# Moving one batch's last norm by half a step and splitting the final copy, turn, sum and store in two, in a one-core gated cross-attention and mixture-of-experts kernel

## What is computed

```python
x = x + tanh(g_xattn[0]) * attention0(layernorm(x), ctx)   # 16 heads of 8
x = x + tanh(g_ffn[0])   * quantised_linear(layernorm(x))  # Hadamard turn, 4-bit rows, ternary weights
x = x + tanh(g_xattn[1]) * attention1(layernorm(x), ctx)   # 16 heads of 64
x = x + tanh(g_ffn[1])   * experts(layernorm(x))           # 32 experts of width 64, top 4, plus a shared expert
```

## Time and profile before

| what | value |
|---|---|
| three runs, median (lowest to highest) | 264.85 us (264.17 to 266.33) |
| the profiled execution's own time | 264.59 us |
| its span in the profile | 262.9 us |
| busy: PE, DVE, ACT, POOL | 95%, 80%, 72%, 69% |
| granted TensorE clock, mean | 0.997 of full speed |

### The profile page before, as it was taken

How to read it: one execution, slowest core, us unless ns; L and a number is a source line. 1 busy time by engine, 2 the same in 40 slices (tenths; PEclk the granted TensorE clock), 3 DMA queues, 4 the chain that set the end, 5 groups by cost and what they waited for, 6 DMA issues and landing times.

```text
span 262.9 us, 6701 instructions
## 1 busy us (share of the span) xinstructions
PE 250.2 (95%) x1899; PEld 198.8 (76%) x1899; DVE 209.8 (80%) x652; ACT 189.0 (72%) x453; POOL 181.7 (69%) x272
## 2 busy tenths in 40 slices
PE   7897999999899999999999999999999999999995
PEld 5574668776667777768777888777887768999994
DVE  3999999999989896799677876777888623996863
ACT  2588899989899787857776767686787654556652
POOL 5667987998899675746744575439767795956661
PEclk9999999999999999999999999999999999999998
DMA  6557463400025566644485766756571051123510
GB/s 197 183 143 281 154 196 86 124 0 4 1 66 119 113 147 146 143 107 103 126 220 122 187 170 172 200 147 162 117 170 42 5 161 40 54 70 126 163 61 20
DMA packets 25475, 31.86 MB, mean 121 GB/s; under 512 B 4000, under 2 KB 18144, under 8 KB 25312
## 3 DMA queue, kind: packets, MB, share of 16 engines
q1 hardware_dynamic: 25008, 31.23, 44.4%
q10 hardware_dynamic: 432, 0.22, 0.3%
HBM read 14.32 MB, written 2.42 MB: 64 GB/s over the span
## 4 chain that ended last, share of the span: by engine, by line
PE 74%; DVE 14%; issue 6%; ACT 3%; DMA 1%; SPq 0%; DVEq 0%; ACTq 0%
PE bank L1325 18%; PE bank L1501 16%; PE bank L1330 6%; PE bank L1463 5%; PE bank L1332 5%; PE bank L1331 5%; PE bank L1464 5%; DVE masked L990 3%; PE bank L1516 3%; PE bank L1457 3%; DVE probsT L1007 2%; PE bank L1591 2%; DMA small<-in_L_ffn_weight 1%; PE bank L1594 1%; PE bank L1592 1%
## 5 line engine op out<-in xcount | busy, mean ns | idle before, releaser
L639 POOL TENSOR_SCALAR probs<-probs,rsum 128x512 f32<-128x512 f32 x128 | 88.3, 697 | 47.9 <-DVE rsum L999 47.3
L786 ACT ACTIVATE probs<-masked,neg_max 128x512 f32<-128x512 f32 x128 | 91.9, 719 | 7.4 <-DVE neg_max L990 7.1
L1325 PE MATMUL bank<-ident,probs 128*128 128x128 f32 x512 | 77.9, 275 | 2.0 <-ACT probsT L795 0.8
L1325 PEld LDWEIGHTS bank<-ident,probs 128*128 128x128 f32 x512 | 59.6, 141 | 15.3 <-issue 7.8
L990 DVE CUSTOM_DVE_ANT_0 masked<-bank,mask 128x512 f32<-128x512 f32 x64 | 43.8, 684 | 17.1 <-PE bank L1464 16.4
L795 ACT ACTIVATE probsT<-bank 128x512 f32<-128x512 f32 x76 | 45.0, 592 | 16.2 <-PE bank L1325 15.9
L1501 PE MATMUL bank<-probsT,val 128*32 128x256 f32 (+1 forms) x512 | 46.6, 384 | 0.0
L990 DVE CUSTOM_DVE_ANT_0 masked<-bank,shared 128x512 f32<-128x512 f32 x64 | 43.3, 677 | 0.8 <-PE bank L1457 0.4
L1007 DVE COPY probsT<-bank 128x512 f32<-128x512 f32 x52 | 35.2, 677 | 4.0 <-PE bank L1325 3.7
L1501 PEld LDWEIGHTS bank<-probsT,val 128*32 128x32 f32 (+1 forms) x512 | 24.4, 123 | 17.2 <-issue 4.2
L1457 PE MATMUL bank<-parts 128*128 128x512 f32 x64 | 31.2, 487 | 1.3 <-DVE neg_max L990 1.1
(11 more groups left out here) (266 smaller groups left out, 519.9 us busy)
## 6 DMA issues: line engine op xcount, KB each, us to landing
k_both<-k_low SPq DMA_DIRECT2D x32, 128.0 KB, 2.5
k_both<-k_high SPq DMA_DIRECT2D x32, 128.0 KB, 2.7
q<-q_split SPq DMA_DIRECT2D x32, 128.0 KB, 2.4
probsT<-staged_gate SPq DMA_DIRECT2D x32, 128.0 KB, 3.0
q<-q_split SPq DMA_DIRECT2D x32, 64.0 KB, 2.2
parts<-staged_k SPq DMA_DIRECT2D x7, 256.0 KB, 2.9
w_flat<-in_w SPq DMA_DIRECT2D x1, 1536.0 KB, 7.5
staged_q<-q_split SPq DMA_DIRECT2D x4, 256.0 KB, 2.6
```

The source lines that it names most:

```text
L639: pool.tensor_scalar(p, p, rsum[:, u % NCOL:u % NCOL + 1], 1.0, ALU.mult, ALU.mult).then_inc(normed, 1)
L786: act.activation(probs[:, u % NP, :], masked[:, u % NS, :], ACT.Exp, scale=-1.0, bias=neg_max[:, c:c + 1], accum_out=sums[:, c:c + 1]).the ...
L1325: ins = pe.transpose(dst[0:rows, t * P:t * P + P], src, ident[:, :])
```

## The change

In the router of batch 1, the norm's turn goes from n = 7 to n = 8, on PE between `up(4, 0)` and `up(4, 1)`, and the logits from n = 8 to n = 9, on PE behind `up(4, 1)` and `down(1)`. On ACT the norm's two copies go from before `high_hid(2)` to behind silu(4), ahead of `high_hid(3)`; the late exponentials stay at n = 10. On DVE `x1_low` goes from before `multiply(3)` to behind `hidden(3)`, and the selection from n = 9 (before `multiply(4)`) to n = 10 (behind `hidden(4)`). Rank and gate turn stay where they are.

At the end, the copy of 128x256 becomes two of 128x128, the turn two single transposes that each wait for their own half and write to two different banks, the sum two of 128x128, and the store two of 64 KB: the first from SP, the second from ACT's queue. The first batch's end is as before.

```diff
--- before.py
+++ after.py
@@ -106,8 +106,8 @@
 Y_DONE = {(k.layer, k.b): k.out_at + 1 for k in BLOCKS if k.g == k.groups - 1}
 
 
-LATE_JOBS = {"ln": 7, "logits": 8, "rank": 11, "turn_gate": 14}
-LATE_ROUTER = {3: (0, 1), 5: (3,), 9: (6, 10), 11: (11, 12)}
+LATE_JOBS = {"ln": 8, "logits": 9, "rank": 11, "turn_gate": 14}
+LATE_ROUTER = {3: (0, 1), 5: (3,), 10: (6, 10), 11: (11, 12)}
 
 
 HIDDEN_AT = {e: (e,) for e in range(2 * STEPS)}
@@ -591,9 +591,13 @@
                                  staged_gate[b, 2 * d:2 * d + 2, h, :].partition_broadcast(HID)).then_inc(gate_loaded[n % GATE_SLOTS], 16)
 
             def store(b):
-                sp.wait_ge(y_used, 3 + b)
-                sp.dma_start(out.rearrange("b (t p) d -> p b t d", p=P)[:, b, :, :],
-                             x_sb[:, NQ * b:NQ * b + NQ, :]).then_inc(stored, 16)
+                if b == 0:
+                    sp.wait_ge(y_used, 3)
+                    sp.dma_start(out.rearrange("b (t p) d -> p b t d", p=P)[:, b, :, :],
+                                 x_sb[:, NQ * b:NQ * b + NQ, :]).then_inc(stored, 16)
+                else:
+                    sp.wait_ge(y_used, 4)
+                    sp.dma_start(out[b, 0:P, :], x_sb[:, NQ * b, :]).then_inc(stored, 16)
 
             sp.wait_ge(job_done, jobs_done(range(8)))
             for b in range(B):
@@ -604,7 +608,7 @@
                     load_gates(b, d)
             for b in range(B):
                 store(b)
-            sp.wait_ge(stored, 16 * B)
+            sp.wait_ge(stored, 16 * (B + 1))
 
 
         @block.gpsimd
@@ -909,7 +913,11 @@
                 act.wait_ge(down_done, (b + 1) * STEPS)
                 if b:
                     act.wait_ge(y_turned, b)
-                act.activation(yT, moe_bank[b][:, 0:SQ], ACT.Copy).then_inc(yT_ready, 1)
+                if b == 0:
+                    act.activation(yT, moe_bank[b][:, 0:SQ], ACT.Copy).then_inc(yT_ready, 1)
+                else:
+                    for t in range(NQ):
+                        act.activation(yT[:, t * P:t * P + P], moe_bank[b][:, t * P:t * P + P], ACT.Copy).then_inc(yT_ready, 1)
 
             for b in range(B):
                 for p in range(HALVES):
@@ -924,9 +932,9 @@
                         if e >= 2:
                             act.wait_ge(hid_ready, e - 1)
                         act.activation(silu[:, e % 2, 0:wide], u_bank[e % 2][:, 0:wide], ACT.Silu).then_inc(silu_ready, 1)
-                        if n + 1 == LATE_JOBS["ln"]:
+                        if n == LATE_JOBS["ln"]:
                             job(("ln", 3, 1))
-                        if n == LATE_JOBS["logits"] + 2:
+                        if n == LATE_JOBS["logits"] + 1:
                             job(("logits", 1))
                         if n == LATE_JOBS["turn_gate"] - 2:
                             job(("turn_gate", 1))
@@ -936,6 +944,8 @@
                         copy_y(0)
             high_hid(2 * STEPS - 1)
             copy_y(1)
+            act.wait_ge(y_used, 5)
+            act.dma_start(out[1, P:SQ, :], x_sb[:, NQ + 1, :]).then_inc(stored, 16)
 
 
         @block.vector
@@ -1314,8 +1324,11 @@
                 dve.wait_ge(down_done, e + 1 - RING)
                 dve.tensor_tensor(hid_low[:, e % RING, 0:cols], hidT[:, e % RING, 0:cols], hid_high[:, e % RING, 0:cols].bitcast(F32),
                                   ALU.subtract).then_inc(last_low_ready, 1)
-            dve.wait_ge(y_turned, 2)
-            add_y(2, 1, 3)
+            for t in range(NQ):
+                x = x_sb[:, NQ + t, :]
+                dve.wait_ge(y_turned, 2 + t)
+                dve.scalar_tensor_tensor(out=x, in0=moe_bank[t][:, 0:P], scalar=tanh_g[:, 3:4], in1=x,
+                                         op0=ALU.mult, op1=ALU.add).then_inc(y_used, 1)
 
 
         @block.tensor
@@ -1599,7 +1612,12 @@
                 pe.wait_ge(yT_ready, b + 1)
                 if b:
                     pe.wait_ge(y_used, 3)
-                turn_tiles(moe_bank[0], [tmp[:, t, :] for t in range(NQ)]).then_inc(y_turned, 1)
+                if b == 0:
+                    turn_tiles(moe_bank[0], [tmp[:, t, :] for t in range(NQ)]).then_inc(y_turned, 1)
+                else:
+                    for t in range(NQ):
+                        pe.wait_ge(yT_ready, 2 + t)
+                        pe.transpose(moe_bank[t][:, 0:P], tmp[:, t, :], ident[:, :]).then_inc(y_turned, 1)
 
             for b in range(B):
                 for p in range(HALVES):
@@ -1617,6 +1635,9 @@
                         up(e, 0, u_bank, u_ready)
                     if n == HALVES:
                         down(QUADS - LAG, "both")
+                    if n == LATE_JOBS["ln"]:
+                        pe.wait_ge(*freed(("logits", 0)))
+                        job(("ln", 3, 1))
                     if p % 2 or p == PAIRS:
                         up(e, 1, v_bank, v_ready)
                         for done in HIDDEN_AT.get(e - LAG, ()):
@@ -1625,9 +1646,8 @@
                     if n == HALVES + 9:
                         turn_y(0)
                     for j in AFTER.get(n, ()):
-                        if j == ("ln", 3, 1):
-                            pe.wait_ge(*freed(("logits", 0)))
-                        job(j)
+                        if j != ("ln", 3, 1):
+                            job(j)
             for e in range(2 * STEPS - LAG, 2 * STEPS - 2):
                 down(e, "both")
             for part in ("high", "low"):
```

## The result

The changed kernel takes 266.18 us (median of 21 runs, 265.33 to 267.02); the kernel before, beside it, took 265.56 us (21 runs, 264.17 to 266.55). The ratio is 1.003, 95% interval 1.0017 to 1.0044: slower by 0.8 us (0.45 to 1.2), inside 1%. The forecast was 265.9 us, 1.05 us more than the median then known. The profiled execution took 266.5 us, its span 264.6 us (before 264.59 and 262.9).

What follows compares the result with a forecast made beforehand. TensorE, busy 95% of the span, was taken as the bound, so only its waits and the end count. 264.59 + 1.4 (router) - 0.35 (end) = 265.65, with 0.26 for the median 265.9 us; range 264.0 to 267.2.

Steps and rivals of the forecast that it cites:

- The late rank: Batch 1's router: the later selection makes the rank on PE start 1.7 us later, at 234.0 against 232.26.
- What comes back: Behind the rank: part of the delay is regained, leaving `multiply(5)`, `down(5)` and all after 1.4 us later.
- The bounds of 0.9 and 1.8: Lower and upper limits, in us, of the router move's forecast loss of 1.4 us.
- The norm's turn: Batch 1's router: PE turns 0.2 us later, ACT's copy `xnT` comes 1.8 us later; `down(1)` gets a new wait.
- The logits' wait: Batch 1's router on PE: the logits start at 229.75, behind a wait of about 0.35 us.
- The end: Halved copy, turn, sum and store: -0.35 us, 0.1 from an earlier last issue and 0.25 from half the data.
- The page's rule against two transfers: Last store: disjoint halves serialize on the same 16 engines, so the landing gains nothing; the end gives only -0.1 us.
- part 2: The kernel's end in halves: forecast -0.35 us, bounds -0.6 and +0.3.
- A: Rival at `down(2)`: the selection ends before PE is through, so the removed waits count; 263.9 us, chance 0.18.
- B: Rival at PE's idle stretch before the rank: the clock falls, costing 2.4 us more; 268.3 us, chance 0.09.
- C: Rival at the end: the second store on ACT's queue lands 1 us later than SP's; 267.1 us, chance 0.08.
- D: Router: smaller loss if the selection or `x1_low` get ahead; 265.2 us, counted inside the likeliest case's 0.65.

Runs made afterwards that it cites:

- rank_late: The changed kernel with the rank two halves later on PE, behind `down(3)`; measured 1.0032 (1.0015 to 1.0049) of the kernel before.
- end_stores_on_sp: The kernel before with the end in halves, both 64 KB stores issued from SP; one execution, 3.57 us from last copy to span's end, for 3.73.
- router_only: The kernel before with all the router's moves of the change and none of the end's; measured 1.0076 (1.0049 to 1.0104) of the kernel before.

## Why the prediction was right

- **The late rank.** Foretold 1.7 us late, with PE idle from 232.4 to 234.0; it was 1.70 us late with 1.40 us shown as idle. The 0.3 us that PE was to give back ahead of `down(5)` it did give back (0.28), but ahead of the gate turn and of `up(9, 0)`; at `down(5)` itself the spacing from the start before is 0.28 us in the old kernel and 0.27 in the new. The step carried because it followed the order of the three engines' lists and took the lengths (0.69 for a product, 2.29 for the selection) from rows.
- **What comes back.** Foretold 1.4 us at `multiply(5)` and `down(5)`; measured 1.40 and 1.42, and 1.44 for the router alone. That this is a bound of its own, and not what is left over from the first, is shown by rank_late. The bounds of 0.9 and 1.8 weren't needed.
- **The norm's turn.** The copy 1.8 us later for a turn 0.2 us later: 1.78 and 0.20. The new wait ahead of `down(1)` was there, 0.41 us shown. The logits' wait was to be about 0.35 us; the profile shows 0.20, and 0.37 beyond the usual spacing from start to start (0.48, less the spacing of 0.11 to 0.12).
- **The end.** The sum -0.35 held (-0.36), but its two terms were mis-sized in opposite directions. The work in halves was to give 0.1 us and gave 0.03, since the first turn starts 0.42 us behind the copy's start (261.65 - 261.23), where I had 0.32: if the first copy was over after 0.27, as I had it (the row shows both copies together), the handover from ScalarE to TensorE took about 0.1 us more than the 0.05 that I had read off the old copy. From there on the lengths were as foretold (0.61 us for both sums, foretold 0.62). The landing was to give 0.25; from the last issue's start to the end it gave 0.33, of which half the data alone is 0.28 (end_stores_on_sp). But that counts only because the second store could be issued at once: on SP it would have come 0.15 us later behind its data. That ACT's queue is worth 0.18 us in the tail wasn't in the prediction, which held it for a risk.
- **The page's rule against two transfers** (the Trainium skill, DMA: Bandwidth & Descriptors, Rules for kernel authors) would have made part 2 -0.1 us. That row speaks of halves by partition, while both stores here cover all 128 partitions, so it bears on this end only by its reason, that the two share the same engines. The trace differs from what I made of it: with the halves ready at different times two stores end 0.31 us sooner than one (3.39 against 3.70). That a second issuing engine saves issue time, as the same table says, the 0.18 us show.
- **The rivals.** A (the selection in time) fell by the row of the rank. B (the clock falls in the hole) didn't come, by the windows; in the one with 0.16 us of PE work the granted clock is 1.00:

```profile
233.00:234.00 1.00, 0.16 (x2) 0.00 (x0) 0.90 (x6) 0.00 (x0) 0.17 (x1) 1.00 0.06 10
234.00:235.00 1.00, 0.44 (x9) 0.47 (x10) 0.38 (x2) 0.49 (x3) 0.00 (x0) 1.00 0.00 1
```

  Whether it couldn't have come isn't shown. The prediction leaned on the end of the old kernel, where the clock fell about 1.2 us after the last transposes. In the changed kernel's own trace it hasn't fallen 1.9 us after them (261.65 + 0.41 = 262.06), in a window without any PE work:

```profile
263.50:264.00 0.50, 0.00 (x0) 0.00 (x0) 0.00 (x0) 0.00 (x0) 0.00 (x0) 1.00 0.49 140
```

  Over the 13 traces the fall behind the last transposes comes after anything from 1.2 to 2.2 us in eight, and not at all up to the end (2.5 to 2.8 us) in five. So 1.2 us was one case of many and no measure for the hole, and two traces with a hole (this one and router_only, both at 1.00) don't tell how likely a fall was. None of the 21 runs came near the 268.3 us of B; the longest was 267.02.

  C (a slow store on ACT's queue) fell by its 1.6 us of landing. D lies inside what was forecast, but neither of its ifs came.
- **The number.** 265.9 us against 266.18, with the kernel before at 265.56 rather than 264.85 in 21 runs. That 265.9 is so near has some luck in it: its start, from three runs, lay 0.7 us under the median of the 21, and its step 0.4 us over the one between the two medians (0.62). The difference is the better test: +1.05 forecast, +0.8 (0.45 to 1.2) measured, +1.10 by the traces from `up(0, 0)`.

## What to carry to other kernels

A visible wait on the busiest engine is worth removing only if what follows isn't due at a fixed time by another chain: here three chains (POOL's low half, the selection, the gates' product ahead of `multiply(5)`) stood within 0.2 us of each other. Up to the last copy, loosening one gave nothing (42.22 us both times) and all three gave 0.2 to 0.45, since the bound went on to the next step; the halved end adds another 0.3 to 0.4. The other two weren't loosened one at a time. When a job is moved half a step on one engine, its copies and consumers move by the whole distance to the next free place in their own engines' lists; read those places first. At a kernel's end, splitting the last store pays by how much data is left behind the last result and by a second free queue to issue it, not by shorter compute.

## What the runs showed of the hardware

ACT's DMA queue, last used in the first 2 us, landed 64 KB in 1.6 us at the end, no slower than SP's; the 4.1 us of its use at the start went with the crowd there. Halving an operation of 128x256 to two of 128x128 made it longer on both engines: 0.48 to 0.61 us on VectorE and 0.38 to 0.45 on ScalarE. And TensorE's granted clock doesn't fall at a fixed distance behind its last work: a hole of 1.68 us between two starts left it at 1.00 in both traces that have one (changed, router_only), and behind the last transposes of 13 traces it fell after 1.24 us at the earliest, after 2.2 at the latest, and in five not within the 2.5 to 2.8 us that were left.
